# Scratch fill, value evacuation and head stacking of a fused two-layer transformer kernel, placed at other points of the schedule

## What is computed

```python
x = x + 0.5 * L0_ffn(layernorm(x))    # attention (not causal), then a mixture of 8 experts, one per token
x = x + L0_attn(layernorm(x))         # causal attention
x = x + 0.5 * L0_ffn(layernorm(x))    # the same weights again
x = x + 0.5 * L1_ffn(layernorm(x))    # 128 -> 512 -> 128, two low-rank variants, relu
x = x + L1_attn(layernorm(x))         # causal attention
x = x + 0.5 * L1_ffn(layernorm(x))
```

```python
q, k, v = (x @ W + b, split into 16 heads)
scores  = einsum('bhid,bhjd->bhij', q, k) / sqrt(8)      # 512 x 512 per head and sequence
attn    = softmax(scores)                                # causal where the layer is causal
out     = einsum('bhij,bhjd->bhid', attn, v) @ W_o + b_o
```

## Time and profile before

| what | value |
|---|---|
| median of three runs | 1199.05 us (1198.54 to 1207.12) |
| the profiled execution, its own time | 1205.25 us |
| its span from first to last instruction | 1203.4 us |
| mean granted TensorE clock | 0.869 of full speed |
| TensorE matmuls busy | 929.8 us (77% of the span) |
| VectorE busy | 769.9 us (64%) |
| ScalarE busy | 668.3 us (56%) |
| GpSimd busy | 310.4 us (26%) |
| exponentials (719) | 896 instructions, 455.8 us |
| pass-one maxima (822 and 813) | 448 instructions, 496.5 us |
| value products (659) | 4352 matmuls, 281.2 us |

### The profile page before, as it was taken

The page is one execution under the profiler, slowest core; times in us unless marked ns, Lnnn a source line. Parts: engine busy times, 40 slices in busy tenths (PEclk is TensorE's granted clock), DMA queues, the critical chain, the costliest instruction groups (busy, mean ns, idle before and its releaser), DMA issues.

```text
span 1203.4 us, 25584 instructions
## 1 busy us (share of the span) xinstructions
PE 929.8 (77%) x9800; PEld 483.8 (40%) x9800; DVE 769.9 (64%) x1288; ACT 668.3 (56%) x1448; POOL 310.4 (26%) x574
## 2 busy tenths in 40 slices
PE   1598998565692798988989998635949579898778
PEld 1123232123591344544323322235936334454345
DVE  6789898325353776777887997233546467777365
ACT  1287888450481376666787887514722237666521
POOL 5542310014343222333314001133420222211010
PEclk8599999785796699999999999756969759999979
DMA  5111136401202211121010100002010031110000
GB/s 165 49 33 50 46 90 82 41 1 44 77 31 71 77 49 34 32 56 37 23 52 20 37 2 2 1 21 77 31 44 1 26 81 49 33 32 4 3 9 27
DMA packets 77261, 49.38 MB, mean 41 GB/s; under 512 B 22242, under 2 KB 74754, under 8 KB 77154
## 3 DMA queue, kind: packets, MB, share of 16 engines
q1 hardware_dynamic: 74658, 42.78, 14.9%
q0 software_dynamic: 2496, 5.13, 1.2%
HBM read 12.72 MB, written 9.21 MB: 18 GB/s over the span
## 4 chain that ended last, share of the span: by engine, by line
PE 54%; ACT 12%; issue 11%; DVE 10%; SPq 5%; POOL 4%; DMA 3%; DVEq 0%; POOLq 0%; ACTq 0%
PE ps L583 14%; PE ps L659 13%; ACT pt L719 9%; PE ps L1349 5%; PE ps L1067 4%; PE ps L1076 4%; DVE negm L822 3%; DVE blockm L813 3%; POOL sorted L1286 3%; PE ps L1337 3%; PE ps L589 2%; PE ps L615 2%; PE ps L667 2%; PE ps L677 2%; ACT ot L725 1%
## 5 line engine op out<-in xcount | busy, mean ns | idle before, releaser
L719 ACT ACTIVATE pt<-ps 128x512 f32<-128x512 f32 (+1 forms) x896 | 455.8, 565 | 196.2 <-PE ps L583 142.0
L822 DVE TENSOR_REDUCE negm<-ps 128x2 f32<-128x1024 f32 x256 | 301.6, 1220 | 52.5 <-PE ps L583 50.9
L659 PE MATMUL ps<-pt,va 128*32 128x256 f32 (+1 forms) x4352 | 281.2, 348 | 52.4 <-ACT ot L725 43.2
L813 DVE TENSOR_REDUCE blockm<-ps 128x8 f32<-128x1024 f32 (+1 forms) x192 | 194.9, 1043 | 74.8 <-PE ps L583 40.3
L583 PE MATMUL ps<-ks,qs 61*128 61x128 bf16 (+2 forms) x1536 | 180.3, 303 | 23.1 <-DVE negm L822 11.0
L583 PE MATMUL ps<-qs,ks 64*128 64x128 bf16 (+3 forms) x1408 | 170.9, 300 | 18.6 <-DMA qs<-mrow 12.2
L659 PEld LDWEIGHTS ps<-pt,va 128*32 128x32 f32 x4352 | 93.9, 110 | 168.3 <-issue 77.4
L583 PEld LDWEIGHTS ps<-ks,qs 61*128 61x128 bf16 x1536 | 56.9, 98 | 182.1 <-issue 111.3
L947 POOL CAST mpart<-negm 128x16 bf16<-128x16 f32 x64 | 13.0, 203 | 369.0 <-PE ps L583 152.6
L583 PEld LDWEIGHTS ps<-qs,ks 64*128 64x128 bf16 x1408 | 60.2, 96 | 70.4 <-ACT pt L719 37.6
L1240 DVE COPY pt<-experts 128x1156 f32 x50 | 38.8, 777 | 70.7 <-DVE upd L1251 37.0
(11 more groups left out here) (156 smaller groups left out, 1136.2 us busy)
## 6 DMA issues: line engine op xcount, KB each, us to landing
qs<-parts SPq DMA_DIRECT2D x80, 128.0 KB
ks<-parts SPq DMA_DIRECT2D x80, 128.0 KB
experts<-in_L_ffn_w SPq DMA_DIRECT2D x16, 256.0 KB
pt<-sorted SPq DMA_DIRECT2D x2, 1225.5 KB, 6.8
sorted<-pad_row SPq DMA_DIRECT2D x6, 384.0 KB, 9.0
qs<-mrow SPq DMA_DIRECT2D x128, 6.0 KB
pt<-y_rows SPq DMA_DIRECT2D x8, 256.0 KB, 3.9
ks<-parts SPq DMA_DIRECT2D x32, 56.0 KB
```

Source lines behind the costliest of these rows:

```text
L659: ins = pe.matmul(pv_bank[32 * j:32 * j + 32, q0:q1], va[n % 2][:, kb, 4 * g + j, 0 if odd else DH + 1:VW - DH - 1 if odd else VW], pt[:, ...
L719: a.activation(pt[:, k_ % NPT, S * s:S * s + width], b_bank(o + s)[:, 0:width], ACT.Exp).then_inc(b_free, 1)
L813: v.tensor_reduce(blockm[:, g % 2, :, t, PLACES[c_]], pair_of(ka)[:, :, 0:width].rearrange("p s (b c) -> p s b c", c=P), AX, ALU.max, nega ...
L822: v.tensor_reduce(negm[:, g % 2, :, t, c_], pair_of(ka), AX, ALU.max, negate=True).then_inc(a_free, 1)
```

## The change

Five edits are made.

1. `late_inputs` is placed at 14.9, that is in the last quad of segment 0, after everything else that SP issues in that segment.
2. `evac` is due one slot earlier, and so are `o`, `onT` and `out`.
3. For the first batch of each segment (`heads`: 0, 4 and 12) the stack DMAs of the keys are issued by ScalarE and those of the queries by SP, and `krem` and `klo` are done by VectorE.
4. The second batch's `hT`, `q`, `k` and what follows them no longer precede the first scores; they stand between the first pass-one slots (`SECOND`, counted in quads before the first quad), and its stacking begins at -1.75. Its `stats`, `rstd` and `norm` still precede.
5. The clearing of `va`, `qs` and `ks` is spread: VectorE keeps `va` 0 and the second pair of `qs` and `ks`, GpSimd takes `va` 1, the third pair and `blockm`, in the pieces of `later_constants` that are called at `SETUPS`. Writing the kept hidden state (`keep`, 922) becomes a job of its own behind the first batch's remainders.

```diff
+HEAD = [("stats", 0), ("rstd", 0), ("norm", 0), ("hT", 0), ("q", 0), ("qrem", 0), ("k", 0), ("krem", 0), ("qmid", 0),
+        ("kmid", 0), ("qlo", 0), ("klo", 0), ("clear", 0), ("v", 0), ("keep", 0), ("stats", 1), ("rstd", 1), ("norm", 1),
+        ("keep", 1)]
+SECOND = [("hT", 1.9), ("q", 1.8), ("qrem", 1.75), ("k", 1.65), ("krem", 1.6), ("qmid", 1.5), ("kmid", 1.4), ("qlo", 1.35),
+          ("klo", 1.3)]
+SETUPS = [-0.95, -0.6, -0.3, 0.1, 1.1, 2.1]
+LATE_INPUTS = 14.9
...
-        for name, before in PREP:
-            at = [-100.0, -50.0][k] if k < 2 and name != "v" or k == 0 else 4 * k - before
-            jobs.append((at, name, n, None))
-        for i, which in enumerate(STACK):
-            at = STACK_EVERY * i
-            jobs.append((-100.0 if k == 0 else at - LEAD if k == 1 else 4 * k - STACK_FROM + at, "stack", n, which))
-    jobs += [(-200.0 if i < LOADS_FIRST else LOADS_FROM + (i - LOADS_FIRST) * LOADS_EVERY, "load", i, None)
-             for i in range(loads)]
+        if k == 0:
+            jobs += [(-100.0, name, batches[k_], None) for name, k_ in HEAD]
+            jobs += [(-50.0, "stack", n, which) for which in STACK]
+            continue
+        jobs += [(-before, name, n, None) for name, before in SECOND] if k == 1 else []
+        jobs += [(4 * k - before, name, n, None) for name, before in PREP if k > 1 or name == "v"]
+        begin = -1.75 if k == 1 else 4 * k - STACK_FROM
+        jobs += [(begin + STACK_EVERY * i, "stack", n, which) for i, which in enumerate(STACK)]
+    for i in range(loads):
+        at = -200.0 if i < LOADS_FIRST else LOADS_FROM + (i - LOADS_FIRST) * LOADS_EVERY
+        jobs.append((at if i < loads - 1 else LATE_INPUTS, "load", i, None))
...
-                    due.append((slot + V_LATER + 2, "evac", n, g // 2))
-                    due.append((slot + V_LATER + 4, "o", n, g // 2))
+                    due.append((slot + V_LATER + 1, "evac", n, g // 2))
+                    due.append((slot + V_LATER + 3, "o", n, g // 2))
...
+                elif name == "stack":
+                    if at[0] == 1 and n in heads:
+                        stack(a, n, at)
...
+                elif name in ("krem", "klo") and n in heads:
+                    remainder(v, name, n)
+                elif name == "clear":
+                    zeros_between(v, 1).then_inc(cleared, 1)
+                    ones_below(v, 1).then_inc(cleared, 1)
...
-        def later_constants(g_):
+        def later_constants(g_, piece):
...
+            if piece == 0:
+                const(empty_values(g_, 1))
                 g_.wait_ge(const_done, done[0])
+                const(one_value(g_, 1))
+            elif piece == 1:
+                const(zeros_between(g_, 2))
+            elif piece == 2:
+                const(ones_below(g_, 2))
...
+                    if not (at[0] == 1 and n in heads):
+                        stack(sp, n, at)
```

More of the change, by code:

```diff
@@ L341, in program @@
         stood_apart = sem("stood_apart")
-        NCONST = 18
+        SETUP_COUNTS = [2, 1, 1, 7, 4, 8]
+        NCONST = sum(SETUP_COUNTS)
         W = [
@@ L437, in program @@
         segment_at = {0: 0, 1: 1, 3: 2}
+        heads = [members[0] for members in segments]
         plans, at_a, at_b, at_step, at_pv, at_m, at_evac, at_quad, pv_of_step = [], {}, {}, {}, {}, {}, {}, {}, {}
@@ L850, in attention_dve @@
                                                ALU.add).then_inc(guard_done, 1)
-        def later_constants(g_):
-            done = [0]
+        def later_constants(g_, piece):
+            done = [sum(SETUP_COUNTS[:piece])]
             def const(ins):
@@ L858, in const @@
                 ins.then_inc(const_done, 1)
-            const(g_.memset(earlier[:, :], 0.0))
-            const(g_.memset(lower_e[:, :, :], 0.0))
-            const(g_.memset(mask_q[:, :, :, :], 0.0))
-            const(g_.memset(mask_k[:, :, :, :], 0.0))
-            const(g_.iota(count_i[:, :], pattern=[[1, SLOTS + AHEAD]], base=0, channel_multiplier=0))
-            const(g_.iota(pref_i[:, :, :], pattern=[[0, TILES], [-1, E]], base=E, channel_multiplier=0))
-            g_.wait_ge(const_done, done[0])
@@ L867, in later_constants @@
-            const(g_.affine_select(out=earlier[:, :], in_=earlier[:, :], compare_op=ALU.is_ge, fill=1.0, base=0,
-                                   pattern=[[-1, P]], channel_multiplier=1))
-            const(g_.affine_select(out=lower_e[:, :, :], in_=lower_e[:, :, :], compare_op=ALU.is_ge, fill=1.0, base=0,
-                                   pattern=[[-1, E], [1, E]], channel_multiplier=0))
-            const(g_.affine_select(out=mask_q[:, :, :, :], in_=mask_q[:, :, :, :], compare_op=ALU.is_ge, fill=MASKED,
-                                   base=0, pattern=[[HALF, 2], [-HALF, 2], [1, P]], channel_multiplier=-1))
@@ L875, in later_constants @@
-            const(g_.affine_select(out=mask_k[:, :, :, :], in_=mask_k[:, :, :, :], compare_op=ALU.is_ge, fill=MASKED,
-                                   base=0, pattern=[[-HALF, 2], [HALF, 2], [-1, P]], channel_multiplier=1))
-            for s in range(2):
-                g_.wait_ge(const_done, done[0])
-                const(g_.tensor_copy(eye[HALF * s:HALF * (s + 1), :, :],
-                                     identf[HALF * s:HALF * (s + 1), HALF * s:HALF * (s + 1)]
-                                     .rearrange("p (o c) -> p o c", o=1).broadcast_to([HALF, TB, HALF])))
@@ new lines, in later_constants, with remainder @@
+            assert done[0] == sum(SETUP_COUNTS[:piece + 1])
+        def remainder(eng, name, n):
+            c_ = 0 if name[0] == "q" else 1
+            if name[1:] == "rem":
+                need(eng, b_free, at_b[(name[0], n, None)] + 1)
+                eng.tensor_tensor(q32[:, c_, :], q32[:, c_, :], parts[:, c_, 0, :],
+                                  ALU.subtract).then_inc(rem_done[c_], 1)
+            else:
+                need(eng, rem_done[c_], n + 1)
+                need(eng, mid_cast[c_], n + 1)
+                eng.tensor_tensor(parts[:, c_, 2, :], q32[:, c_, :], parts[:, c_, 1, :],
+                                  ALU.subtract).then_inc(lo_done[c_], 1)
@@ L918, in attention_pool @@
                         g_.tensor_tensor(a_rstd2[:, :], a_tmp[:, :], a_rstd[:, :], ALU.mult).then_inc(at_rstd, 1)
-                elif name == "norm":
+                elif name == "keep":
                     if w["moe"]:
@@ L1461, in _ @@
         def _(v):
-            ones_below(v, 0)
+            ones_below(v, 0).then_inc(cleared, 1)
             for kind, w, cnt in phases:
```

136 lines of the change are left out of this document (77 added, 59 removed).

## The result

| | before | after |
|---|---|---|
| median of four runs | 1198.95 us | 1132.02 us (1130.96 to 1133.24) |
| the profiled execution, its own time | 1205.25 us | 1130.96 us |
| its span | 1203.4 us | 1129.0 us |
| mean granted TensorE clock | 0.869 | 0.897 |
| ratio of the times, 95% interval | | 0.943 (0.939 to 0.947) |

The change gains 67 us. The forecast was 1148, the range 1136 to 1168: the sign was right and the gain too small by 16 us, outside the range.

The account below looks back on a forecast made before the run. No engine bounds the kernel alone (TensorE holds 54% of the chain), so only waits ending on the path could pay. Gains of 13.4 + 32.5 + 1.8 + 3.4 + 0 = 51.1 us from 1199.05 gave 1148 us, range 1136 to 1168.

Parts of the forecast that it names:

- Scratch fill: End of segment 0: with no maxima queued behind the fill on SP, 13.4 us less (12.2 to 15).
- That rival: End of segment 0: the fill delays the first scatter or holds other transfers, 13 us lost, 1161 us; chance 0.04.
- Copy-out one slot earlier: Slot loop: TensorE waits 1.12 us less at each of 29 copy-outs, 32.5 us in all (0 to 43.2).
- Clock: Pairs slowed by TensorE's lower clock behind a pause: three found, 3.6 us; half taken, 1.8 us (0 to 3.6).
- Head of segment 0: Start of segment 0: first maxima at about 32.5 instead of 39.53, fourth ending at 40.7; 3.4 us less (-1 to 7.0).
- Heads of segments 1 and 2: Starts of segments 1 and 2: earlier stack DMAs offset by projections between scores; 0 us (-2.8 to +3 each).
- the 16 and 19 that I set: Segment 1, first stack DMA to third maximum, 18.2 us before: over 19 the heads lose, under 16 they gain.
- issue in turn from two queues: Heads of segments 1 and 2: stack DMAs still issue one after the other, 2.8 us lost each, 1153.5 us; chance 0.12.
- Half taken: Slot loop: only half the relief at the copy-outs arrives, 16 us less gain, 1164 us; chance 0.16.
- copy-out without effect: Slot loop: ScalarE waits for the pair's last product and TensorE for ScalarE as before, 1180 us; chance 0.05.
- The slower one: Slot loop: TensorE loses its clock through whole pairs, 13.3 us per causal pair, 1214 us from about five; chance 0.02.

Follow-up runs that it names:

- copy-out moved alone: The kernel before with only evac, o, onT and out due one slot earlier; 1154.68 us, ratio 0.958.
- fill put back: The changed kernel with the scratch fill at its old place, issued by SP; 1146.04 us, ratio 0.954.
- fill alone: The kernel before with only the scratch fill moved to the last quad of segment 0; 1187.99 us, ratio 0.984.
- copy-out back: The changed kernel with evac, o, onT and out due at their old slots again; 1185.07 us, ratio 0.982.
- the kernels on the heads: The changed kernel with all stack DMAs on SP (1139.73 us), second-batch projections ahead of the first scores (1135.59), or both (1137.44).
- the kernel with four extra copies: The changed kernel with four extra ScalarE copies of the same bank into a spare tile ahead of each copy-out; 1258.02 us, ratio 1.043.

## Why the prediction was wrong

By its own steps:

- **Scratch fill, 13.4:** right. The change's window is 13.9 us shorter than with the copy-out moved alone (35.54 - 21.68), 11.6 shorter than with the fill put back, whose ratio says 14. The fill stayed hidden: its last DMA is issued at 232.22, the weights' load behind it at 251.73, and the first scatter comes at 258.29 with [13.31 <-issue], as before with 13.36. That rival falls.
- **Copy-out one slot earlier, 29 x 1.12 = 32.5:** right for the copy-out, and short by its followers. I compare each window after with the shortest reading of the same window at clock 1.00 in three traces that have the pause (before, fill alone, copy-out back). 23 slot windows have one and are 27.8 us shorter, four more by their likes 3.8, the fill's window 1.1 (22.76 - 21.68), the first copy-out of each segment about 1.17 earlier (86.67 - 85.50 with the copy-out alone; 1.2 and 1.3 in segments 1 and 2 against the kernel with the copy-out back), 3.5 in all: 36 us. The 28th window, the last of all, is at clock 0.87 in all three; its 1.0 us goes to the clock. Of the 36, 4.6 are `o`, `onT` and `out`, which I cost at nothing without saying so; so the copy-out itself gave 31 to 32.
- **Clock, 1.8:** this is the step that failed, a term of the sum mis-sized by a factor of seven to nine (1.8 forecast, 12 to 16 measured). I wrote "I find three like it, 3.6 us" and took half. Read window by window, the trace of before had 10 of 28 slot windows below 1.00, and by the same comparison (595.2 against 553.2 + 31.5) they cost 10.5 us in it; 14 to 15 in each of the two other traces with the pause. TensorE's busy time in the 28 windows says the same without any comparison of likes: 522.5 us after, 533.4 before, 537.5 and 536.1 in the other two. The fill's window adds up to 1.5, as in its twin (24.21 at 0.93, 22.76 at 1.00), which makes 12 to 16 in all. And not half but all of it goes with the pause, since at 0.25 and at 0.74 us the clock hardly ever falls. The rows were in reach: I had looked at the few windows that fitted a point and not at all of them.
- **Head of segment 0, 3.4:** right: 4.4 to the first copy-out, of which 1.17 is edit 2; 2.2 of the rest is edit 4 and 1.0 what stays in all the kernels on the heads (the clearing, `krem` and `klo` on VectorE). First maxima at 32.65 (predicted 32.5), the third and fourth scores behind q and k at 36.84 and 39.38 (37.0 and 39.5), the fourth maximum ends at about 41.
- **Heads of segments 1 and 2, 0:** nearly right, 0.7 and 1.3 of gain by one trace each, with a scatter of nearly 1. First stack DMA to third maximum is 371.09 - 354.09 = 17.0 us, between the 16 and 19 that I set. The issues ran at 0.61 to 0.85 us each on ScalarE.

In sum: 13.4 + 36 + 12 to 16 + 3.2 + 2.0 = 67 to 71, against 67 measured by the medians, 69 by the ratio, and 51.1 forecast. Of the 16 missing, at least 10 are the clock, about 4 the followers and 2 the heads.

The rivals: issue in turn from two queues is refuted by the rows above, for the queues of SP and ScalarE. The Trainium skill (page Perfetto Trace Analysis, section "DMA Instruction — HWDGE (DVE, Sync)"), which I had put beside it, states the shared generator for the VectorE and SyncE sequencers, and adds in a note that the mechanism is the same whichever engines issue. Between SyncE and ScalarE this trace doesn't agree: 0.88 and 0.85 us a DMA side by side, and no turns taken. Half taken, and copy-out without effect, fall with the 0.25 us waits. The slower one looked at the right quantity and had its direction wrong: the clock does decide 12 to 16 us here, but in favour of whoever removes the pause, and the kernel with four extra copies (1258 us) shows its price.

What stays open: why a pause of the same length lowers the clock in one window and not in its twin (10, 13, 12 and 12 of 28 in four traces, not the same ones), and what sets the scatter of the mixture stretches.

## What to carry to other kernels

A short pause of the fullest engine that comes back in every round has two prices: its length, and the clock behind it. Count the second over all rounds (windows cut at the same event, with their granted clock), not from examples. Here it went whole once the pauses were 0.74 us or shorter. When a step is moved, price its followers too, and test edits of one head together: here a second queue and the projections' new place gain a little as a pair in segments 1 and 2, where the new place alone loses 2.3 to 2.4 us and the queue alone gives 0.3 and 1.4.

## What the runs showed of the hardware

- In a window at 0.91, the clock falls to half 0.7 us behind the end of a pause of 1.47 us and is back some 3.4 us later. It doesn't do so behind every such pause. The loss is steep in the length of the pause: 29 pauses of 0.25 or 0.74 us leave 0 or 1 of 28 windows below 1.00, of 1.37 us 12, of 2.63 us 27.
- With the pause gone the loop is very regular: the 28 windows sum to 553.1 to 553.2 us in seven kernels, while with it they read 595.2, 599.2 and 598.9.
- The DMA queues of SP and ScalarE issue at the same time, at 0.61 to 0.88 us a DMA in segments 1 and 2, with little slowing (0.87 instead of 0.70 for one pair on SP). In segment 0 one DMA of ScalarE took 1.43 us.
- Large transfers delay small ones of another queue: with 3 MB from GpSimd's queue under way, the 6 KB `mrow` DMAs that SP issued from 194.75 and 207.99 let TensorE go on at 204.09 and 218.96 only, and it waited 6.67 us.
